# Hybrid block on one core: which engine writes the normalised rows of attention A

## The chip, the cores and the metric

One NeuronCore of one Trainium2 chip. The time is device microseconds (us) of one execution of the whole program, as the median of several runs. The program is a chain of four layers on 8 batches of 512 tokens with 128 features: linear attention A, a mixture of experts, a logarithmic attention B, and the mixture of experts once more. All of it is fp32.

## The reference, cut to what matters

```python
def layernorm(x, eps=1e-5):
    return (x - mean(x)) / sqrt(var(x) + eps)

def attn_a(x):                       # x is the normalised input, 8 x 512 x 128
    q, k, v = split(x @ W_qkv)       # 16 heads of 8
    q, k = rope(q), rope(k)
    q_feat, k_feat = elu(q * SCALE) + 1, elu(k) + 1
    kv, k_sum = k_feat.T @ v, k_feat.sum(tokens)
    out = (q_feat @ kv) / max(q_feat @ k_sum, 1e-6)
    return out @ W_out

x = x + attn_a(layernorm(x))
x = x + ffn(layernorm(x))            # shared expert + 2 of 8 experts
x = x + attn_b(layernorm(x))
x = x + ffn(layernorm(x))
```

The change concerns the first line of the chain alone: the layernorm in front of attention A.

## The kernel before, in words

Each engine (TensorE, VectorE, ScalarE, GpSimd, SyncE) has its own program, written out by hand, and runs it strictly in the order written. Semaphores tie the programs together: an instruction can raise one when it is done, and `wait_ge` holds an engine until one has reached a value. Nothing else sets the order of the work, so a wait holds up everything that stands behind it on its engine.

Attention A is a software pipeline over the 8 batches, in steps b = 1 to 9 (`A_STEPS`). In step b the engines finish the attention of batch b - 1 (named b in the calls below that ask for b > 1), work on the keys of the next, and prepare the queries of batch b + 1. x lies in SBUF as x_res, 4 tiles of 128 tokens per batch. A batch n is normalised like this:

- VectorE: statistics of the four tiles (`vector_stats`, L186), mean and variance into mean_var (L191), variance plus epsilon into var_eps (L193).
- GpSimd: rstd = var_eps to the power -0.5 (`pool_rstd`, L197).
- VectorE: four `tensor_scalar` of 128x128, x_hat = (x - mean) * rstd (`vector_hat`, L203). Mean and rstd are one number per partition (token). It waits for rstd and, so that x_hat is free again, for the transposes of the batch before (`turned`).
- TensorE: four transposes of x_hat (`tensor_turn`, L210); ScalarE copies the result to xT (L216), from which the projections read.

In step b TensorE's order is: tokens projected to v and k (L282), the router's logits of an earlier batch (L757), the sums of keys and values (`a_sums`, L249), the transposes of x_hat for batch b + 1 (`tensor_turn`, L210), the numerators (`a_numerators`, L256), the projection of q (L277, L278), transposes and the output projection (L266, L270). The numerators therefore stand behind the transposes, and the transposes wait for x_hat.

VectorE's order in step b (`a_vector_step`) is: the bias of the expert layer's norm (L1216, steps 3 to 6, waits for GpSimd's f_rstd), the four rows of x_hat (L203), `a_keep_heads` (L323, L324, waits for the sums), the rotation of k (L346), the router's logits (L1245), `a_divide` (L329, L331, L334, waits for the numerators), the features of q (L358), statistics of batch b + 2, the features of k (L358), the rotation of the next q (L346), the residual add (L341), and the statistics of the expert layer's norm (L1205 to L1210).

GpSimd's order in step b (`attn_a_pool`) is: the second half of the rotation of k (`a_add_turned`, L352), rstd of batch b + 2 (L197), the second half of the rotation of the next q (L352), f_rstd of the expert layer (L1029, in steps 2 to 5), and in steps 4, 5 and 6 a piece of preparation for the experts: a cast of 128x256 (L474) in step 4, a cast and a subtraction of 128x256 (L478, L480) in steps 5 and 6. After step 8 GpSimd sends the tokens to their experts by indirect DMA (L1047), as soon as VectorE has worked out the rows (rows_of, L1384).

Of the kernel before, what the change touches and what calls it, by code (L numbers as in the profile page):

```python
# [21 lines left out]
B, T, D = 8, 512, 128  # L22
H, HD = 16, 8
TT = T // 128
# [73 lines left out]
def build(nc, x_in, ins, out):  # L98

    ctx = ExitStack()  # L100
    with ctx:
        def sb(name, shape, dtype=F32):
            return ctx.enter_context(nc.sbuf_tensor(name, shape, dtype))

        def sem(name):
            return ctx.enter_context(nc.semaphore(name))
# [13 lines left out]
        mean_var = sb("mean_var", [128, TT, 2])  # L120
        var_eps = sb("var_eps", [128, TT])
        neg_half = sb("neg_half", [128, TT])
        rstd = sb("rstd", [128, TT])
        x_hat = sb("x_hat", [128, TT, D])
        xT = sb("xT", [128, T])

        def xs(n, t=0, tiles=1):

            return x_res[:, bass.ds((n - 1) * (TT * D) + t * D, tiles * D)]
# [6 lines left out]
        def signals(engine, prefix, passed=1.0, **steps):  # L136


            made = [(sem(f"{prefix}_{name}"), k) for name, k in steps.items()]
            starts[engine] += [(s, int(k * passed)) for s, k in made if int(k * passed)]  # L140
            return [s for s, _ in made]
# [29 lines left out]
        class Norm:  # L171
# [2 lines left out]

            def __init__(self, name, used, used_count, used_before=0):
                self.used, self.used_count, self.used_before = used, used_count, used_before
                self.stats_done, self.mean_done, self.var_ready, self.hat_ready = signals(
                    "vector", name, stats_done=TT, mean_done=TT, var_ready=1, hat_ready=TT)
                self.rstd_ready, = signals("pool", name, rstd_ready=1)
                self.turned, = signals("tensor", name, turned=1)  # L180
                self.xT_ready, = signals("scalar", name, xT_ready=1)
                self.go = sem(f"{name}_go")
# [13 lines left out]
                p.wait_ge(self.var_ready, n + 1)  # L196
                nc.gpsimd.tensor_tensor(rstd[:], var_eps[:], neg_half[:], ALU.pow).then_inc(self.rstd_ready, 1)  # L197

            def vector_hat(self, v, n):
                v.wait_ge(self.rstd_ready, n + 1)  # L200
                v.wait_ge(self.turned, n)
                for t in range(TT):
                    nc.vector.tensor_scalar(x_hat[:, t, :], xs(n, t), mean_var[:, t, 0:1], rstd[:, t:t + 1],  # L203
                                            ALU.subtract, ALU.mult).then_inc(self.hat_ready, 1)

            def tensor_turn(self, pe, n, to):
# [21 lines left out]
        na = Norm("a", a_kv, 1)  # L228
# [90 lines left out]
        def a_keep_heads(v, b):  # L319

            v.wait_ge(a_sum, b)
            v.wait_ge(a_num, b - 1)
            nc.vector.tensor_tensor(kv_bd[:, 0:D], bank(5, D), const["same_head"][:], ALU.mult).then_inc(a_bd, 1)  # L323
            nc.vector.tensor_scalar(kv_bd[:, D:D + H], const["head_mask"][:], psum[:, 5, D:D + 1], None,  # L324
                                    ALU.mult).then_inc(a_bd, 1)

        def a_divide(v, b):
            v.wait_ge(a_num, b)
            nc.vector.tensor_scalar(den[:], num_den(5)[:, :, D:D + H], EPS, None, ALU.max).then_inc(a_den, 1)  # L329
            v.wait_ge(a_den, b)  # L330
            nc.vector.reciprocal(rec[:], den[:]).then_inc(a_rec, 1)  # L331
            v.wait_ge(a_rec, b)
            v.wait_ge(a_oT, b - 1)
            nc.vector.tensor_tensor(o_tok[:].rearrange("p t (h d) -> p t h d", d=HD),  # L334
                                    num_den(5)[:, :, 0:D].rearrange("p t (h d) -> p t h d", d=HD),
                                    rec[:].unsqueeze(3).broadcast_to([128, TT, H, HD]),
                                    ALU.mult).then_inc(a_o, 1)
# [5 lines left out]
        def a_rotate(v, b, n, prod, first_bank, table):  # L343

            v.wait_ge(a_feat, 2 * b + n - 1)
            nc.vector.tensor_tensor(prod, psum[:, first_bank:first_bank + 2, :], table, ALU.mult).then_inc(a_prod, 1)  # L346

        def a_add_turned(p, b, n):

            prod = (q_prod, k_prod)[n]  # L350
            p.wait_ge(a_prod, 2 * b + n + 1)
            nc.gpsimd.tensor_tensor(prod[:, 0, :], prod[:, 0, :], prod[:, 1, :], ALU.add).then_inc(a_rope, 1)  # L352

        def a_feature(v, b, n, prod, e, feat):

            v.wait_ge(a_exp, 2 * b + n + 1)
            v.wait_ge((a_num, a_sum)[n], b)
            nc.vector.scalar_tensor_tensor(feat, prod[:, 0, :], 0.0, e, ALU.max, ALU.add).then_inc(a_feat, 1)  # L358
# [5 lines left out]
        def a_stats(v, n):  # L364
            v.wait_ge(loaded_x[min(n, 4) - 1], 16 * (B - 3) if n == 4 else 16)
            na.vector_stats(v, n)

        def a_vector_step(v, b):
            if 1 <= b - AHEAD <= ffn_1.early:
                ffn_1.vector_bias(v, b - AHEAD)  # L370
            if b < B:
                na.vector_hat(v, b + 1)
            if b > 1:
                a_keep_heads(v, b)
            if b <= B:
                v.wait_ge(a_kv, b + 1)
                a_rotate(v, b, 1, k_prod, 2, rope_k)
            if 1 <= b - AHEAD - 1 <= ffn_1.early:
                ffn_1.vector_logits_of(v, b - AHEAD - 1)
            if b > 1:  # L380
                a_divide(v, b)
            if b <= B:
                a_feature(v, b, 0, q_prod, q_exp, q_feat)
            if b == 7:
                ffn_1.vector_first(v, 0)
            if b == 8:
                ffn_1.vector_gates(v, 0)
                ffn_1.vector_pages(v, 0)
                ffn_1.vector_rows(v, 0)
            if b + 2 <= B:  # L390
                a_stats(v, b + 2)
            if b <= B:
                a_feature(v, b, 1, k_prod, k_exp, k_feat)
            if 1 <= b - AHEAD <= ffn_1.early:
                ffn_1.vector_low(v, b - AHEAD)
            if b < B:
                a_rotate_q(v, b + 1)
            if b == B + 1:
                ffn_1.vector_bias(v, ffn_1.first_late)
                ffn_1.vector_stats(v, ffn_1.first_late + 1)  # L400
            if b > 1:
                a_add(v, b)
            if 1 <= b - AHEAD + 1 <= ffn_1.early:
                ffn_1.vector_stats(v, b - AHEAD + 1)
            if b == 7:
                ffn_1.vector_second(v, 0)
            if b == 8:
                ffn_1.vector_stats(v, ffn_1.first_late)
                ffn_1.vector_experts(v, 0)

        def attn_a_vector(v):
            a_stats(v, 1)
            na.vector_hat(v, 1)
            v.wait_ge(loaded_first, 16 * len(first_loads))
            a_rotate_q(v, 1)
            a_stats(v, 2)
            for b in A_STEPS:
                a_vector_step(v, b)
# [39 lines left out]
        def attn_a_pool(p):  # L458

            na.pool_rstd(p, 1)  # L460
            a_add_turned(p, 1, 0)
            nc.gpsimd.memset(x_res[:, B * TT * D:], 0.0).then_inc(set_zero, 1)
            na.pool_rstd(p, 2)
            for b in range(1, B + 1):
                a_add_turned(p, b, 1)
                if b + 2 <= B:
                    na.pool_rstd(p, b + 2)
                if b < B:
                    a_add_turned(p, b + 1, 0)
                if 1 <= b - AHEAD + 1 <= ffn_1.early:  # L470
                    ffn_1.pool_rstd(p, b - AHEAD + 1)
                if b == 4:
                    p.wait_ge(loaded, 16 * len(rest_loads))
                    nc.gpsimd.tensor_copy(const["earlier"][:], earlier_room).then_inc(split_low, 1)  # L474
                if b in (5, 6):
                    g = b - 5
                    whole, high, low = w["w_expert"][:, g * INNER:(g + 1) * INNER], w_shared[:, g, 0, :], w_shared[:, g, 1, :]
                    nc.gpsimd.tensor_copy(high, whole).then_inc(split_high, 1)  # L478
                    p.wait_ge(split_high, g + 1)
                    nc.gpsimd.tensor_tensor(low, whole, high.bitcast(F32), ALU.subtract).then_inc(split_low, 1)  # L480
            sends = (0, 4, 8, 12, 14, 2 * ffn_1.tiles(0))
            for k in range(len(sends) - 1):
                ffn_1.send(p, 0, sends[k], sends[k + 1])
                if ffn_1.first_late + k <= B:
                    ffn_1.pool_rstd(p, ffn_1.first_late + k)
# [1945 lines left out]
```

## Time and profile before

| | |
|---|---|
| median of 3 runs | 1026.62 us (1026.45 to 1029.6) |
| profiled execution, its own time | 1028.43 us |
| its span, first to last instruction | 1026.6 us |
| busy share: TensorE, VectorE, ScalarE, GpSimd | 80%, 72%, 55%, 57% |
| attention A within it | 0 to about 125 us |

In the rows below PE is TensorE's matmul, PEld its weight load, DVE VectorE, ACT ScalarE, POOL GpSimd. L203 is line 203 of the kernel. In a timeline row the first number is the start in us, the second the duration of the group, x4 the number of instructions in it; in brackets stands how long the engine was idle before it and what it waited for ("issue" is a wait that the profile can't name).

### The profile page before, as it was taken

Reading aid. Unit: us, or ns where it says so; the run is one execution under the profiler, and the core shown is the slowest. Engines: PE = TensorE matmul, PEld = TensorE weight load, DVE = VectorE, ACT = ScalarE, POOL = GpSimd, SP = SyncE. Lnnn points to the kernel's source line nnn. Section 1 sums busy time; section 2 is a strip of 40 time slices with the busy share of each in tenths; the row PEclk is TensorE's granted clock in tenths of the full one; section 3 lists DMA queues with packets and bytes.
Section 4 is the critical chain, followed back from the end, with each engine's and each line's share of the span. In section 5 each row is a group of like instructions: output and inputs, shape, how many; then the busy total and the mean of one; then the engine's idle time right before and its main releaser. Section 6 shows DMA issues by size and latency. Waiting matters only on the chain. (4 is left out here: it accounts for less than half of the span.)

```text
span 1026.6 us, 19542 instructions
## 1 busy us (share of the span) xinstructions
PE 822.4 (80%) x6459; PEld 546.7 (53%) x6459; DVE 734.5 (72%) x1506; ACT 568.4 (55%) x805; POOL 589.0 (57%) x815
## 2 busy tenths in 40 slices
PE   4887587899997777888888888979795678899890
PEld 2676466798985333333333333333352267898880
DVE  3888845455564658899999998999779645565574
ACT  1454142233345577989898989998763251233230
POOL 2343585881274566665644444455317877788783
PEclk9899678999997787999999999999877598999996
DMA  9990012123338477474837473732210121132443
GB/s 270 303 131 1 19 36 72 52 81 114 101 92 239 140 215 225 121 221 127 227 100 220 111 226 104 231 99 63 62 42 24 34 75 39 40 102 81 135 136 119
DMA packets 114402, 124.00 MB, mean 121 GB/s; under 512 B 13329, under 2 KB 76561, under 8 KB 114177
## 3 DMA queue, kind: packets, MB, share of 16 engines
q1 hardware_dynamic: 96512, 100.80, 35.8%
q0 software_dynamic: 8416, 17.29, 5.4%
q10 hardware_dynamic: 9376, 4.65, 1.6%
q8 instruction: 56, 0.92, 0.4%
q14 instruction: 42, 0.34, 0.1%
HBM read 59.97 MB, written 62.72 MB: 120 GB/s over the span
## 5 line engine op out<-in xcount | busy, mean ns | idle before, releaser
L2070 DVE TENSOR_SCALAR ring_b<-psum 128x1024 int32<-128x1024 int32 x160 | 194.2, 1217 | 25.1 <-PE psum L1765 23.9
L1930 ACT ACTIVATE ring_a<-psum 128x1024 f32<-128x1024 f32 x160 | 162.4, 1021 | 47.3 <-PE psum L1765 45.8
L1936 ACT ACTIVATE ring_b<-ring_b 128x1024 f32<-128x1024 f32 x160 | 168.7, 1055 | 34.5 <-DVE ring_b L2070 34.1
L2198 POOL TENSOR_SCALAR_AFFINE_SELECT ring_b<-ring_b 128x512 f32<-128x512 f32 (+1 forms) x112 | 80.3, 730 | 171.6 <-ACT ring_b L1936 171.3
L1765 PE MATMUL psum<-stacks 32*128 32x128 f32 (+3 forms) x1024 | 99.8, 389 | 59.6 <-DVE ring_b L2070 39.8
L1765 PEld LDWEIGHTS psum<-stacks 32*128 32x128 f32 x1024 | 57.6, 195 | 164.6 <-ACT ring_a L1930 75.7
L2062 DVE TENSOR_SCALAR ring_a<-ring_a 128x1024 f32<-128x1024 f32 x160 | 119.3, 751 | 11.7 <-ACT ring_a L1930 11.7
L949 ACT ACTIVATE ring_b<-psum 128x512 f32<-128x512 f32 x72 | 42.6, 592 | 116.5 <-PE psum L834 116.5
L1818 PE MATMUL psum<-ring_b,values 128*32 128x256 f32 (+3 forms) x1024 | 96.5, 488 | 8.2 <-POOL ring_b L2198 8.2
L1797 PE MATMUL psum<-ring_a,ones_s 128*32 128x256 f32 (+3 forms) x1024 | 93.0, 473 | 10.1 <-POOL ring_a L2198 9.2
L1448 DVE TENSOR_TENSOR ring_b<-psum,ring_b 128x512 f32<-128x512 f32 x72 | 49.2, 683 | 67.7 <-ACT ring_b L949 67.7
L1092 POOL DMA_INDIRECT r_rows<-y_sorted,rows_of x64 | 67.4, 1053 | 51.8 <-DMA y_sorted<-y_out 39.5
L848 PE MATMUL psum<-w_expert,ring_b 128*128 x568 | 85.6, 285 | 13.8 <-ACT y_out L965 9.0
L2198 POOL TENSOR_SCALAR_AFFINE_SELECT ring_a<-ring_a 128x512 f32<-128x512 f32 (+1 forms) x112 | 79.6, 725 | 22.0 <-DVE ring_a L2062 21.9
L848 PEld LDWEIGHTS psum<-w_expert,ring_b 128*128 128x128 f32 x568 | 72.5, 193 | 21.3 <-issue 21.0
L1071 POOL DMA_INDIRECT y_token<-y_out,token_of x71 | 71.5, 1007 | 21.4 <-POOL pause_room L492 19.9
L1047 POOL DMA_INDIRECT x_sorted<-r_rows,rows_of x64 | 64.0, 1001 | 31.0 <-POOL pause_room L492 15.5
L834 PE MATMUL psum<-ring_a,ring_b 128*128 128x128 f32 x576 | 73.7, 283 | 5.3 <-issue 3.7
L492 POOL MEMSET pause_room<- 128x256 f32 x220 | 75.6, 344 | 0.2
L1047 POOL DMA_INDIRECT x_marked<-r_rows,rows_of x64 | 63.5, 992 | 18.9 <-POOL pause_room L492 16.0
L834 PEld LDWEIGHTS psum<-ring_a,ring_b 128*128 128x128 f32 x576 | 70.6, 200 | 6.4 <-issue 4.6
L834 PE MATMUL psum<-ring_a,v_tok 128*128 128x128 f32 x560 | 68.6, 275 | 0.0
(220 smaller groups left out, 1480.5 us busy)
## 6 DMA issues: line engine op xcount, KB each, us to landing
stack_q<-parts SPq DMA_DIRECT2D x32, 256.0 KB
stack_ky<-parts SPq DMA_DIRECT2D x32, 256.0 KB
stacks<-stack_q SPq DMA_DIRECT2D x64, 128.0 KB, 3.4
stacks<-stack_ky SPq DMA_DIRECT2D x64, 128.0 KB, 3.9
stack_k<-parts SPq DMA_DIRECT2D x32, 256.0 KB
stacks<-stack_k SPq DMA_DIRECT2D x64, 128.0 KB, 3.0
stack_qr<-parts SPq DMA_DIRECT2D x32, 256.0 KB
stacks<-stack_qr SPq DMA_DIRECT2D x64, 128.0 KB, 2.6
```

The lines of the kernel that those rows point to most:

```text
L492: nc.gpsimd.memset(pause_room[:], 0.0).then_inc(paused, 1)
L834: mm = nc.tensor.matmul(bank(2 * (k % 2) + g)[:, at:at + 128], w_pages[i % 4][:, g * INNER + c * 128:g * INNER + (c + 1) * 128], x_turned[ ...
L848: mm = nc.tensor.matmul(tiles(bank(4))[:, i % 4, :], hidden[:, self.items.index(("pair", j)) % 8, at:at + 128], w["w_expert"][:, bass.ds(s ...
L1047: nc.gpsimd.indirect_dma_start(out=out, out_offset=bass.IndirectOffsetOnAxis(ap=rows_of[:, n, at + t:at + t + 1], axis=0), in_=row, in_off ...
L1765: mm = nc.tensor.matmul(bank(2 * pair + j % 2)[:, column:column + width], keys[rows, s, kb * 128:(kb + 1) * 128], queries[rows, s, q0:q0 + ...
L1797: mm = nc.tensor.matmul(psum[32 * j:32 * j + 32, 4, q0:q0 + width], ones_s[:, s, :], exps[:, n % RING, j, column:column + width], start=i ...
L1818: mm = nc.tensor.matmul(psum[32 * j:32 * j + 32, into, q0:q0 + width], values[:, b % 2, kb, 4 * j + s, :], ring[:, m % RING, j, column:col ...
L1930: nc.scalar.activation(exps[:, n % RING, 2 * u:2 * u + 2, :], psum[:, first:first + 2, :], ACT.Exp, scale=SCALE).then_inc(self.exp, 1)
L1936: nc.scalar.activation(part, part, ACT.Ln, bias=1.0).then_inc(self.ln, 1)
L2062: nc.vector.tensor_scalar(part, part, CLIP_LO, CLIP_HI, ALU.max, ALU.min).then_inc(self.clip, 1)
L2070: nc.vector.tensor_scalar(ring[:, m % RING, HEADS_B[u][0]:HEADS_B[u][1] + 1, :].bitcast(I32), psum[:, first:first + 2, :].bitcast(I32), 0x ...
L2198: ins = nc.gpsimd.affine_select(out=part, in_=part, pattern=[[0, part.ap[1][1]], [1, 128]], compare_op=ALU.is_ge, fill=0.0, base=0, channe ...
```

## The change

The four instructions that write x_hat go from VectorE to GpSimd, with the same operands and the same two waits. On GpSimd they stand at the head of step b, in front of the second half of the rotation of k; for batch 1 they stand right behind its rstd. The semaphore hat_ready is now raised by GpSimd. Lines after L371 move up by two or three numbers.

```diff
@@ class Norm
-                self.stats_done, self.mean_done, self.var_ready, self.hat_ready = signals(
-                    "vector", name, stats_done=TT, mean_done=TT, var_ready=1, hat_ready=TT)
-                self.rstd_ready, = signals("pool", name, rstd_ready=1)
+                self.stats_done, self.mean_done, self.var_ready = signals(
+                    "vector", name, stats_done=TT, mean_done=TT, var_ready=1)
+                self.rstd_ready, self.hat_ready = signals("pool", name, rstd_ready=1, hat_ready=TT)
...
-            def vector_hat(self, v, n):
-                v.wait_ge(self.rstd_ready, n + 1)
-                v.wait_ge(self.turned, n)
+            def pool_hat(self, p, n):
+                p.wait_ge(self.rstd_ready, n + 1)
+                p.wait_ge(self.turned, n)
                 for t in range(TT):
-                    nc.vector.tensor_scalar(x_hat[:, t, :], xs(n, t), mean_var[:, t, 0:1], rstd[:, t:t + 1],
+                    nc.gpsimd.tensor_scalar(x_hat[:, t, :], xs(n, t), mean_var[:, t, 0:1], rstd[:, t:t + 1],
                                             ALU.subtract, ALU.mult).then_inc(self.hat_ready, 1)
@@ def a_vector_step(v, b)
-            if b < B:
-                na.vector_hat(v, b + 1)
@@ def attn_a_vector(v)
             a_stats(v, 1)
-            na.vector_hat(v, 1)
@@ def attn_a_pool(p)
             na.pool_rstd(p, 1)
+            na.pool_hat(p, 1)
             a_add_turned(p, 1, 0)
             nc.gpsimd.memset(x_res[:, B * TT * D:], 0.0).then_inc(set_zero, 1)
             na.pool_rstd(p, 2)
             for b in range(1, B + 1):
+                if b < B:
+                    na.pool_hat(p, b + 1)
                 a_add_turned(p, b, 1)
```

What this does to the order on GpSimd in steps 5 to 7 (- as before, + as changed):

```order
 L1029 TENSOR_TENSOR f_rstd<-f_var_eps,neg_half 128x4
 L474 CAST earlier<-values 128x256
+L203 TENSOR_SCALAR x_hat<-x_res,mean_var,rstd 128x128 x4
 L352 TENSOR_TENSOR ring_a<-ring_a 128x512
 L197 TENSOR_TENSOR rstd<-var_eps,neg_half 128x4
...
 L478 CAST w_shared<-w_expert 128x256
 L480 TENSOR_TENSOR w_shared<-w_expert,w_shared 128x256
+L203 TENSOR_SCALAR x_hat<-x_res,mean_var,rstd 128x128 x4
 L352 TENSOR_TENSOR ring_a<-ring_a 128x512
 L197 TENSOR_TENSOR rstd<-var_eps,neg_half 128x4
```

The rows of x_hat now stand behind f_rstd of the expert layer and behind the pieces for the experts, which GpSimd issues at the end of the step before.

On VectorE, at the head of each of the steps 3 to 6:

```order
 L1210 TENSOR_SCALAR f_var_eps<-f_mean_var 128x4
 L1216 SCALAR_TENSOR_TENSOR f_nbias<-f_mean_var,f_rstd 128x4
-L203 TENSOR_SCALAR x_hat<-x_res,mean_var,rstd 128x128 x4
 L323 TENSOR_TENSOR ring_b<-psum,same_head 128x128
 L324 TENSOR_SCALAR ring_b<-head_mask,psum 128x16
```

The bias is followed at once by the two instructions of `a_keep_heads`. TensorE's and ScalarE's orders are the same in both kernels.

## Rows read from the trace of the kernel before

**Rows 1.** Engines by stretch: start:end, length, busy PE, PEld, DVE, ACT, POOL, clock, DMA
```profile
42.00:97.00 55.00, 44.98 (x308) 36.73 (x308) 47.37 (x142) 28.14 (x56) 22.65 (x22) 0.97 0.68 101
```

**Rows 2.** Timeline, step 5
```profile
66.18 1.02 POOL L1029 TENSOR_TENSOR f_rstd<-f_var_eps,neg_half 128x4 f32<-128x4 f32 x1 [0.84 <-DVE f_var_eps L1210]
...
67.16 0.40 POOL L474 CAST earlier<-values 128x256 fp32r<-128x256 f32 x1
67.23 0.34 DVE L1216 SCALAR_TENSOR_TENSOR f_nbias<-f_mean_var,f_rstd 128x4 f32<-128x4 f32 x1 [1.13 <-POOL f_rstd L1029]
67.49 1.11 DVE L203 TENSOR_SCALAR x_hat<-x_res,mean_var,rstd 128x128 f32<-128x128 f32 x4
...
68.70 0.63 PE L210 MATMUL psum<-identity,x_hat 128*128 128x128 f32 x4 [1.20 <-issue]
...
70.35 0.23 DVE L329 TENSOR_SCALAR ring_b<-psum 128x64 f32<-128x64 f32 x1 [0.18 <-PE psum L256]
```

**Rows 3.** Timeline, steps 3 (first two) and 4
```profile
40.98 1.02 POOL L1029 TENSOR_TENSOR f_rstd<-f_var_eps,neg_half 128x4 f32<-128x4 f32 x1 [0.86 <-DVE f_var_eps L1210]
...
42.12 1.11 DVE L203 TENSOR_SCALAR x_hat<-x_res,mean_var,rstd 128x128 f32<-128x128 f32 x4
...
53.97 1.02 POOL L1029 TENSOR_TENSOR f_rstd<-f_var_eps,neg_half 128x4 f32<-128x4 f32 x1 [0.85 <-DVE f_var_eps L1210]
...
54.94 1.14 PE L249 MATMUL psum<-values,ring_a 128*128 128x129 f32 x8
...
55.10 1.12 DVE L203 TENSOR_SCALAR x_hat<-x_res,mean_var,rstd 128x128 f32<-128x128 f32 x4
...
57.97 0.22 DVE L329 TENSOR_SCALAR ring_b<-psum 128x64 f32<-128x64 f32 x1 [0.18 <-PE psum L256]
```

**Rows 4.** Prices: two copies in a row; GpSimd's copy and addition (ns min/median/max)
```profile
402.80 0.53 POOL L2211 COPY values<-v_tok 128x128 f32<-128x128 f32 x2
...
L2211 POOL COPY values<-v_tok x4: 282/287/814, 401.8 to 403.0; 128x128 f32<-128x128 f32 x4
...
L352 POOL TENSOR_TENSOR ring_a<-ring_a x13: 1264/1269/1276, 32.7 to 106.4; 128x512 f32<-128x512 f32 x13
```

**Rows 5.** Timeline, batch 1 (first two) and steps 1 and 2
```profile
6.78 1.11 DVE L203 TENSOR_SCALAR x_hat<-x_res,mean_var,rstd 128x128 f32<-128x128 f32 x4 [1.24 <-POOL rstd L197]
...
9.69 1.09 PE L210 MATMUL psum<-identity,x_hat 128*128 128x128 f32 x4 [9.69 <-DMA head_mask<-in_head_mask]
...
20.23 1.03 POOL L197 TENSOR_TENSOR rstd<-var_eps,neg_half 128x4 f32<-128x4 f32 x1
...
21.29 1.11 DVE L203 TENSOR_SCALAR x_hat<-x_res,mean_var,rstd 128x128 f32<-128x128 f32 x4 [1.15 <-POOL rstd L197]
...
23.46 0.68 DVE L358 SCALAR_TENSOR_TENSOR ring_a<-ring_a 128x512 f32<-128x512 f32 x1
23.62 1.64 POOL L352 TENSOR_TENSOR ring_a<-ring_a 128x512 f32<-128x512 f32 x1 [2.36 <-DVE ring_a L346]
...
28.54 1.30 POOL L352 TENSOR_TENSOR ring_a<-ring_a 128x512 f32<-128x512 f32 x1 [1.77 <-DVE ring_a L346]
...
31.70 0.66 PE L210 MATMUL psum<-identity,x_hat 128*128 128x128 f32 x4 [0.64 <-ACT values L436]
```

**Rows 6.** Timeline, steps 6 (first three) and 7
```profile
78.57 1.02 POOL L1029 TENSOR_TENSOR f_rstd<-f_var_eps,neg_half 128x4 f32<-128x4 f32 x1 [0.85 <-DVE f_var_eps L1210]
...
79.88 1.51 DVE L203 TENSOR_SCALAR x_hat<-x_res,mean_var,rstd 128x128 f32<-128x128 f32 x4
80.03 0.78 POOL L480 TENSOR_TENSOR w_shared<-w_expert,w_shared 128x256 fp32r<-128x256 f32 x1
...
90.93 0.73 POOL L480 TENSOR_TENSOR w_shared<-w_expert,w_shared 128x256 fp32r<-128x256 f32 x1
...
94.49 0.23 DVE L329 TENSOR_SCALAR ring_b<-psum 128x64 f32<-128x64 f32 x1
```

**Rows 7.** Timeline, after step 8: the start of GpSimd's sends
```profile
114.57 1.34 POOL L1047 DMA_INDIRECT x_sorted<-r_rows,rows_of  x1 [6.87 <-DVE rows_of L1384]
```

## The prediction

> **What bounds the kernel now.** I read the busy time by stretch first. In steps 3 to 7 of attention A VectorE is busy 47.4 of 55 us, GpSimd 22.7, TensorE 45.0 [rows 1]. So 1.1 us a step taken off VectorE looks like a gain, and GpSimd seems to have room. A busy share does not say what ends last, though, so I read the timeline of single steps next, at the place of the edit. Step 5 [rows 2] goes so: f_rstd on GpSimd ends at 67.20; VectorE, which had waited 1.13 us for it, does the bias and then the four rows of x_hat, until 68.60; TensorE, idle for 1.20 us, begins the transposes at 68.70; and VectorE's division (L329) begins at 70.35, after an idle 0.18 us, when the numerators are there. From the end of x_hat to the division is 1.75 us. In step 4 it is the same: x_hat ends at 56.22, the division begins at 57.97, again 1.75 us later [rows 3]. That is the chain to look at: f_rstd, x_hat, transposes, numerators (which stand behind the transposes on TensorE), division. Whatever VectorE does between x_hat and the division (keeping the heads, rotating k) must be done by then, but doing it earlier does not bring the division forward. Behind the division VectorE's order goes on to the next statistics, and so to the next f_rstd.
>
> So the time is decided by **when x_hat ends**, not by which engine is relieved. Last comes what lies behind: GpSimd waits 6.87 us for rows_of of VectorE before it can send the first tokens at 114.57 [rows 7]. GpSimd's chain of sends starts there, so I let a shift of attention A pass to the end in full.
>
> **The change, part by part.** VectorE loses four instructions in batch 1 and in steps 1 to 7: eight times 1.1 us or more. GpSimd gains the same 32 instructions. No DMA moves. The two waits go along: rstd is written by GpSimd itself one place or more ahead, and `turned` of the batch before has long been raised, since that batch was already projected; both cost about nothing. What is queued behind the four rows on GpSimd is the second half of the rotation of k, which has to wait for VectorE's rotation anyway.
>
> *Price h of the four rows on GpSimd.* The trace of before has no `tensor_scalar` on GpSimd, so I bound it. Nearest from below is its copy of 128x128: one takes 0.29 us, two in a row 0.53, hence one more every 0.24; four take 0.29 + 3 x 0.24 = 1.0 us [rows 4]. From above its two-tensor operations: 1.27 us for 512 columns [rows 4], about 0.75 for 256 [rows 6], so 0.52 for 256 columns and 0.49 for an operation of 128; four take 2.0. x_hat reads one tensor, as the copy does, but has two arithmetic operations and two numbers per partition to fetch. I take 0.4 a piece, above the middle: h = 1.6, between 1.0 and 2.0. VectorE does the four in 1.11 [rows 2].
>
> The Trainium skill (GPSIMD Engine Reference, section 8, Key points) says that for elementwise work VectorE is structurally about twice as fast. By that the four rows would take 2.2 us, an estimate from that page, and the sum below would be 7.8 us instead of 3.9. For one input the copy's row speaks against it (0.24 us a piece, where VectorE's x_hat takes 1.11 / 4 = 0.28); the operation itself no row here shows.
>
> *Step by step*, the end of x_hat before against the end with h = 1.6:
>
> - Batch 1: VectorE began at 6.78, when rstd was there; with h = 1.6 x_hat ends at 8.4 instead of 7.9, and TensorE waits until 9.69 for a weight's DMA [rows 5]. Nothing, up to h = 2.9.
> - Step 1: rstd ends at 21.26, x_hat ended at 22.40 [rows 5]; now 21.26 + 1.6 = 22.86. VectorE, without its wait of 1.15 and its 1.11 us, comes to the features of q (L358, an operation on two SBUF tensors) about 2.2 us earlier than its 23.46, which is in the middle of GpSimd's rows. How the two get along is seen at 23.46: L358 of 0.68 us had just begun, and GpSimd's addition took 1.64 us in place of 1.27 [rows 4, 5]. It was held until L358 ended. I add 0.6 (bounds 0 and 0.7). Loss 1.06. All that follows in steps 1 and 2 hangs on it: transposes, projection, rotation of q, its sum on GpSimd, the exponentials.
> - Step 2: x_hat now follows the addition of 28.54 + 1.30 on GpSimd: 29.84 + 1.6 = 31.4, where the transposes had waited until 31.70 for ScalarE's copy [rows 5]. Both shift alike; cover 0.3 us. Nothing.
> - Step 3: f_rstd ends at 42.00, x_hat ended at 43.23 [rows 3]; now 43.60. Loss 0.37.
> - Step 4: f_rstd ends at 54.99, x_hat ended at 56.22 [rows 3]; now 56.59. Loss 0.37.
> - Step 5: the cast stands between; it ends at 67.56, now 69.16 against 68.60 [rows 2]. Loss 0.56.
> - Step 6: cast and subtraction stand between, and end at 80.81; now 82.41 against 81.39 [rows 6]. Loss 1.02. Here the head of the step is 1.2 us later on GpSimd than on VectorE, whatever h is.
> - Step 7: the second subtraction ends at 91.66; now 93.26, and the division 1.75 later at 95.01 against 94.49 [rows 6]. Loss 0.52.
>
> Sum 1.06 + 0.37 + 0.37 + 0.56 + 1.02 + 0.52 = **3.9 us**. VectorE's saving stands in this sum at nothing: it becomes idle time in front of the division. Smaller holds of GpSimd by the tiny L1216 and L324, 0.1 or so a step, I leave out. With h = 1.0 each of the six falls by 0.6, except that step 4 gains nothing, since the sums of keys and values end only at 56.08 there and VectorE needs them before the numerators [rows 3], and step 7 returns to its old limit: 0.46 - 0.23 + 0 - 0.04 + 0.42 + 0 = 0.6 us. With h = 2.0: 3.9 + 6 x 0.4 + 0.1 in step 2 = 6.4 us.
>
> The profiled execution took 1028.43 us, of which 1026.6 are its span; it would become 1032.3. The median of the runs shown is 1026.62, lower by 1.8, and I forecast against it: 1026.62 + 3.9 = **1030.5 us**.
>
> **The rivals.**
>
> *Not slower: GpSimd's rows at the price of its copy.* h = 1.0 and the loss is 0.6: 1027.2 us. For it: one tensor input, like the copy. Against it: two more operands. It decides below h = 1.46, where the sum, 3.9 - 6 x 0.14, falls to 0.3% (3.1 us), about what a measurement of this kernel can tell from no change. Chance 0.2, and part of my forecast's own spread ends there too.
>
> *Twice VectorE's price or more.* h = 2.2, by the rows a little above the two-tensor addition: 3.9 + 6 x 0.6 + 0.3 in step 2 = 7.8, so 1034.4 us. For it: GpSimd's addition takes 1.27 us on 512 columns. Against it: the copy, which at 0.24 us a piece is no slower than VectorE's own rows of x_hat. Chance 0.2.
>
> *Faster: what VectorE is spared counts.* If the division did not hang on x_hat, seven steps of 1.1 us would come off: 7.8 us, 1018.8. For it: VectorE's 86% in steps 3 to 7. Against it: the 1.75 us repeated in steps 4 and 5, with the numerators behind the transposes on TensorE. It decides only where GpSimd has x_hat done well before VectorE had it, and GpSimd cannot begin before f_rstd ends, 1.2 to 1.4 us before VectorE was done in steps 3 to 5. Chance 0.07.
>
> *That the rows do not stand where the change says.* The order shows them on GpSimd, behind f_rstd and the casts, so they are there; but "head of the step" is later in time on GpSimd than on VectorE, which is in the sum. A remaining 0.03 goes to things not seen.
>
> **How the numbers follow.** Forecast 0.5, copy price 0.2, double price 0.2, freed VectorE 0.07, rest 0.03. The likeliest is 1030.5. The range goes from 1026.4, just under no change and the copy price, to 1035.0, just over the double price; outside it lie the freed VectorE and part of the rest, and a tail of each price. Slower by over 0.3%: 0.36 of the forecast's 0.5, 0.2 of the double price and a little of the rest: 0.57. Within: 0.14 + 0.2 + 0.01: 0.35. Faster: 0.08.
>
> **What would show it.** In the changed profile the four rows L203 on GpSimd should span 1.3 to 1.9 us, beginning right behind f_rstd in steps 3 and 4 and behind the cast or subtraction in steps 5 to 7; the division should come 1.75 us after their end in each; VectorE should be idle in front of it by about 1 us; and the first send should begin about 4 us later than 114.57. In step 1 the rows should be stretched by VectorE's L358. I am wrong if the division comes well before 1.75 us after x_hat (then VectorE's saving counts), if the rows take 1.0 us or over 2, or if the later part of the program does not carry the shift of the first send to the end.

## The result, and the profile after

The changed kernel takes 1047.89 us in the median (1046.25 to 1053.84, 4 runs) against 1028.11 us before (1026.45 to 1031.25, 4 runs). The ratio is 1.0212, 95% interval 1.0169 to 1.0254: slower by about 20 us. I had forecast slower, by 3.9 us, with 1035.0 as the upper end. The direction was right, the size wrong by a factor of five.

The first row to look at is the one that the trace of before could not have: the price of x_hat on GpSimd (ns min/median/max of one instruction).

```profile
L203 POOL TENSOR_SCALAR x_hat<-x_res,mean_var,rstd x32: 787/797/1319, 6.6 to 112.7; 128x128 f32<-128x128 f32 x32
```

0.79 us a row, where I had taken 0.4 and had put 0.49 as the upper bound [rows 4]. Step 5 of the changed kernel, in order of time, answers to [rows 2]:

```profile
77.64 1.02 POOL L1029 TENSOR_TENSOR f_rstd<-f_var_eps,neg_half 128x4 f32<-128x4 f32 x1 [0.85 <-DVE f_var_eps L1210]
...
78.62 0.40 POOL L474 CAST earlier<-values 128x256 fp32r<-128x256 f32 x1
78.69 0.34 DVE L1216 SCALAR_TENSOR_TENSOR f_nbias<-f_mean_var,f_rstd 128x4 f32<-128x4 f32 x1 [1.13 <-POOL f_rstd L1029]
79.01 3.14 POOL L203 TENSOR_SCALAR x_hat<-x_res,mean_var,rstd 128x128 f32<-128x128 f32 x4
...
82.25 0.63 PE L210 MATMUL psum<-identity,x_hat 128*128 128x128 f32 x4 [3.07 <-issue]
82.71 1.25 PE L256 MATMUL psum<-ring_b,ring_a 128*128 128x144 f32 x8
...
83.99 0.22 DVE L329 TENSOR_SCALAR ring_b<-psum 128x64 f32<-128x64 f32 x1 [3.12 <-PE psum L256]
```

The chain is the forecast one: f_rstd, cast, x_hat, transposes, numerators, division. x_hat ends at 82.15, the division begins 1.84 us later (1.75 before). What VectorE was spared, and the time by which x_hat comes later, stand as idle time in front of the division: 3.12 us in place of 0.18 [rows 2]. What differs from the forecast in this step is that x_hat takes 3.14 instead of 1.6 us.

Step 3 shows a second loss, which the forecast does not have:

```profile
47.10 3.14 POOL L203 TENSOR_SCALAR x_hat<-x_res,mean_var,rstd 128x128 f32<-128x128 f32 x4
...
50.34 1.09 PE L210 MATMUL psum<-identity,x_hat 128*128 128x128 f32 x4 [4.21 <-issue]
...
51.22 2.13 PE L256 MATMUL psum<-ring_b,ring_a 128*128 128x144 f32 x8
...
53.38 0.23 DVE L329 TENSOR_SCALAR ring_b<-psum 128x64 f32<-128x64 f32 x1 [4.60 <-PE psum L256]
```

Here the division comes 3.14 us after x_hat's end at 50.24, because the transposes take 1.09 and the numerators 2.13 us in place of 0.63 and 1.25. TensorE's clock says why (stretches of the changed kernel; the number behind the busy times is the granted clock, as a share of full speed):

```profile
47.00:50.30 3.30, 0.00 (x0) 0.00 (x0) 1.64 (x4) 0.03 (x1) 3.30 (x6) 0.88 1.22 163
50.30:53.40 3.10, 3.06 (x13) 3.09 (x14) 0.02 (x1) 1.94 (x5) 1.17 (x1) 0.50 1.25 147
...
82.20:84.00 1.80, 1.75 (x13) 1.79 (x14) 0.01 (x1) 1.09 (x3) 1.18 (x1) 0.89 0.00 0
...
98.20:101.30 3.10, 3.02 (x13) 3.05 (x14) 0.00 (x0) 1.90 (x5) 1.22 (x1) 0.50 0.03 5
```

TensorE does nothing from 47.0 to 50.3, waiting for x_hat, and works at 0.50, its lower level of 1.2 GHz, behind that. It is the same in steps 4 (0.52) and 6; in steps 5 and 7 the clock stays up and the 1.8 us hold. The length of the wait alone does not decide it: TensorE was idle for 2.14 us in front of the transposes in step 4, and for 3.07 in step 5.

Step 1 shows both the stretch that the forecast has (x_hat beside VectorE's L358) and a low clock that it does not have:

```profile
21.72 0.68 DVE L358 SCALAR_TENSOR_TENSOR ring_a<-ring_a 128x512 f32<-128x512 f32 x1
21.75 3.65 POOL L203 TENSOR_SCALAR x_hat<-x_res,mean_var,rstd 128x128 f32<-128x128 f32 x4
...
25.50 1.02 PE L210 MATMUL psum<-identity,x_hat 128*128 128x128 f32 x4 [4.96 <-issue]
```

The transposes took 0.63 us here in the kernel before. The clock is 0.53 from 25.4 to 28.5 and 0.50 from 28.5 to 32.0; in the kernel before it was 0.81 and 0.69 from 22.4 to 25.4 and from 25.4 to 29.0.

The loss is made in attention A and stays: the first send of GpSimd begins at 134.67 in place of 114.57 [rows 7], 20.1 us later.

```profile
134.67 1.38 POOL L1047 DMA_INDIRECT x_sorted<-r_rows,rows_of  x1 [6.86 <-DVE rows_of L1384]
```

### The profile page after: what moved, and what is told of

Its sections match the earlier page's. It is cut to its first block and busy times, and to the rows that moved or that the text cites. A ratio compares the mean times of both kernels' runs of the same rounds, so it can differ in the third digit from the quotient of the medians.

```text
span 1044.5 us, 19542 instructions
## 1 busy us (share of the span) xinstructions
PE 825.5 (79%) x6459; PEld 551.4 (53%) x6459; DVE 723.3 (69%) x1474; ACT 568.3 (54%) x805; POOL 614.0 (59%) x847
```

## The experiments

The theory after the first look: the chain and its steps are as forecast; the loss of 20 us is the price of a row (0.79 in place of 0.4) plus TensorE's clock behind the longer wait. The rivals: GpSimd's work costs wherever it stands, by quarrelling with VectorE over the memory; or VectorE's time sets the step after all.

The begin of the division in each step, and of the first send, in us, for the kernels that matter below ("filler" is e3_filler, "swap" e8_swap):

| step | before | changed | filler | swap |
|---|---|---|---|---|
| 2 | 33.37 | 38.47 | 38.37 | 33.81 |
| 3 | 45.08 | 53.38 | 51.87 | 44.38 |
| 4 | 57.97 | 69.42 | 65.96 | 55.78 |
| 5 | 70.35 | 83.99 | 80.41 | 67.19 |
| 6 | 83.15 | 101.32 | 95.77 | 78.99 |
| 7 | 94.49 | 115.25 | 109.82 | 90.39 |
| first send | 114.57 | 134.67 | 129.2 | 112.2 |

### What a row costs by itself (e1_prices)

```diff
 na.pool_rstd(p, 1)
+room = r_rows[:, 2100:3540]
+x0, m0, r0 = xs(1), neg_half[:, 0:1], neg_half[:, 1:2]
+nc.gpsimd.tensor_scalar(room[:, 0:128], x0, m0, r0, ALU.subtract, ALU.mult)
+nc.gpsimd.tensor_scalar(room[:, 128:256], x0, m0, r0, ALU.subtract, ALU.mult)
+nc.gpsimd.tensor_scalar(room[:, 256:384], x0, 0.5, 2.0, ALU.subtract, ALU.mult)
+nc.gpsimd.tensor_scalar(room[:, 384:512], x0, r0, None, ALU.mult)
+nc.gpsimd.tensor_scalar(room[:, 512:640], x0, 2.0, None, ALU.mult)
+nc.gpsimd.tensor_scalar(room[:, 640:672], x_res[:, 0:32], m0, r0, ALU.subtract, ALU.mult)
+nc.gpsimd.tensor_scalar(room[:, 672:1184], x_res[:, 0:512], m0, r0, ALU.subtract, ALU.mult)
+nc.gpsimd.tensor_copy(room[:, 1184:1312], x0)
+nc.gpsimd.tensor_tensor(room[:, 1312:1440], x0, x0, ALU.subtract)
```

> The kernel before, with nine extra GpSimd instructions on scratch memory at about 7 us, where GpSimd has nothing to do and VectorE is idle as well. What they write is not used. Theory A (the price is the instruction's own): a tensor_scalar of 128x128 with mean and rstd as per-partition operands takes 0.79 us here too, as in the changed kernel. Theory B (the price comes from VectorE, which shares a way to the memory, or from operands just written): 0.3 to 0.5 us here. If A, the other forms tell what costs: with two constants in place of the two operands, with one operation, with 32 and with 512 columns. If the columns cost, 512 columns take about four times as long as 128; if the instruction costs a fixed sum, 512 columns in one instruction are far below four of 128. Copy 0.29 us, subtraction of two 128x128 tensors about 0.5.

GpSimd's timeline, in the order of the edit:

```profile
6.44 0.80 POOL L463 TENSOR_SCALAR r_rows<-x_res,neg_half 128x128 f32<-128x128 f32 x1
7.24 0.89 POOL L464 TENSOR_SCALAR r_rows<-x_res,neg_half 128x128 f32<-128x128 f32 x1
8.11 0.63 POOL L465 TENSOR_SCALAR r_rows<-x_res 128x128 f32<-128x128 f32 x1
8.74 0.60 POOL L466 TENSOR_SCALAR r_rows<-x_res,neg_half 128x128 f32<-128x128 f32 x1
9.32 0.52 POOL L467 TENSOR_SCALAR r_rows<-x_res 128x128 f32<-128x128 f32 x1
9.84 0.47 POOL L468 TENSOR_SCALAR r_rows<-x_res,neg_half 128x32 f32<-128x32 f32 x1
10.29 2.06 POOL L469 TENSOR_SCALAR r_rows<-x_res,neg_half 128x512 f32<-128x512 f32 x1
12.31 0.28 POOL L470 COPY r_rows<-x_res 128x128 f32<-128x128 f32 x1
12.58 0.39 POOL L471 TENSOR_TENSOR r_rows<-x_res 128x128 f32<-128x128 f32 x1
```

Meanwhile on VectorE, which then does nothing until 13 us:

```profile
6.45 1.41 DVE L203 TENSOR_SCALAR x_hat<-x_res,mean_var,rstd 128x128 f32<-128x128 f32 x4 [1.24 <-POOL rstd L197]
```

The first two rows, 0.80 and 0.89 us, ran beside VectorE's x_hat (until 7.86), against what was expected, and so do not tell the theories apart. The instructions behind them ran with VectorE idle. There the same form grows from 0.47 to 2.06 us from 32 to 512 columns, 3.3 ns a column, on top of about 0.36 (0.47 - 32 x 3.3 ns), which makes 0.79 for 128 columns. So theory A: it is the instruction's own price, not contention. Constants in place of the two operands take off about 0.2, one operation instead of two again about 0.1. The subtraction of two tensors, which I had used as the upper bound, takes 0.39: on GpSimd the operation with per-partition operands is the dearer one, not the one with two tensors.

### The rows a step earlier on GpSimd (e2_early)

```diff
 na.pool_rstd(p, 2)
+na.pool_hat(p, 2)
 for b in range(1, B + 1):
-    if b < B:
-        na.pool_hat(p, b + 1)
     a_add_turned(p, b, 1)
     if b + 2 <= B:
         na.pool_rstd(p, b + 2)
+        na.pool_hat(p, b + 2)
```

> The changed kernel, with GpSimd's four rows of x_hat right behind the rstd that they need, a step earlier, in place of at the head of the step behind f_rstd. Price and number of the instructions are the same. Theory A (x_hat's end is what counts): the transposes no longer wait for x_hat from step 2 on; only batch 1, step 1 and some delay of what stands behind the rows on GpSimd remain. 1028 to 1035 us, most of the loss of 20 us gone. Theory B (GpSimd's 25 us more of work, or its quarrel with VectorE over the memory, is the cost wherever it stands): 1042 us or more.

1038.84 us in the median, ratio 1.0117 (1.0051 to 1.0184); first send at 126.0. About half of the loss goes with the same instructions at the same price (the first send comes 8.7 us earlier than in the changed kernel), so the place matters, and theory B falls; but 10 us stay, where theory A had 0 to 7. Step 5 shows one part of where they come from:

```profile
72.11 1.27 POOL L352 TENSOR_TENSOR ring_a<-ring_a 128x512 f32<-128x512 f32 x1
73.34 1.03 POOL L1029 TENSOR_TENSOR f_rstd<-f_var_eps,neg_half 128x4 f32<-128x4 f32 x1
...
74.40 0.34 DVE L1216 SCALAR_TENSOR_TENSOR f_nbias<-f_mean_var,f_rstd 128x4 f32<-128x4 f32 x1 [2.50 <-POOL f_rstd L1029]
75.23 0.42 PEld L210 LDWEIGHTS psum<-identity,x_hat 128*128 128x128 f32 x4 [2.20 <-ACT values L433]
```

x_hat is early now, and the transposes wait for ScalarE's copy. But the 3.1 us of rows push what stands behind them on GpSimd: the rotation of q (L352), for which that copy waits, and f_rstd, for which VectorE waits 2.50 us in place of 1.13. Moved forward, the price is paid at another place of the same loop. Another part is the clock: in steps 3 and 6 it was 0.50 and the transposes and numerators took 1.11 and 2.13 us, in step 5 0.66 and 1.15. How the 10 us divide between the two was not measured.

### TensorE kept at work before x_hat comes (e3_filler, e9_after_again, e10_filler_again)

```diff
 pe.wait_ge(a_v, b + 1)
+for _ in range(2 if 1 < b < 7 else 0):
+    nc.tensor.matmul(bank(7), w["w_a"][:, 0:D], xT[:], start=True, stop=True)
 na.tensor_turn(pe, b + 1, 7)
```

> The changed kernel, with two extra projections (their result is overwritten) on TensorE in front of its wait for x_hat in steps 2 to 6. Theory A (part of the loss is TensorE's clock, which was granted at 0.5 for about 3 us behind the wait in steps 3, 4 and 6): the clock stays up, the way from x_hat's end to the division falls from 3.1 to about 1.8 us in these three steps, and the time is 3 to 5 us below the changed kernel's, so about 1043 to 1045. Theory B (the clock there covers nothing that is waited for, or does not follow the idle time): no gain, 1047 to 1049.

1046.41 us, ratio 1.0178 (1.0122 to 1.0234), first send at 129.2. In attention A it is theory A: from step 3 to the first send 5.5 us are won (table). At the end it lies between the two theories and could not be told from the scatter, so I ran it again beside the changed kernel.

> The changed kernel as it is, beside the next one on the same chip. Both theories: 1046 to 1050 us, first send at 134 to 135.

> The changed kernel with two extra projections in front of TensorE's wait for x_hat in steps 2 to 6, once more and beside the changed kernel itself. In the first look its first send came at 129.2 instead of 134.7, but the program ended only 1.5 us earlier, within the scatter of the runs. Theory A (the 5 us won by the clock in attention A reach the end, and that execution lost them to chance later): the first send again at about 129, and the median 3 to 6 us below the changed kernel's of the same call. Theory B (they are given back later): first send at about 129, medians within 2 us.

1049.08 us for the changed kernel (ratio 1.0210, 1.0164 to 1.0256) and 1043.99 with the filler (1.0174, 1.0123 to 1.0224), first sends at 134.4 and 129.2. The medians differ by 5.1 us, as the first sends do; the intervals of the two ratios overlap, but five of the six executions with the filler took less than any of the six without it. That is theory A. Step 3 with the filler (e10), and its clock:

```profile
47.06 1.98 PE L302 MATMUL psum<-xT,w_a 128*128 128x512 f32 x4 [0.95 <-ACT values L435]
...
50.26 0.66 PE L210 MATMUL psum<-identity,x_hat 128*128 128x128 f32 x4 [1.21 <-POOL x_hat L203]
...
50.75 1.15 PE L256 MATMUL psum<-ring_b,ring_a 128*128 128x144 f32 x8
...
51.93 0.23 DVE L331 TENSOR_SCALAR ring_b<-psum 128x64 f32<-128x64 f32 x1 [3.17 <-PE psum L256]
```

```profile
47.00:50.30 3.30, 2.03 (x5) 0.72 (x5) 1.64 (x4) 0.01 (x1) 3.30 (x6) 1.00 1.18 212
50.30:53.40 3.10, 3.10 (x16) 2.14 (x17) 1.40 (x4) 2.45 (x6) 1.14 (x1) 1.00 1.23 161
```

With 2 us of useless work in front of the wait the clock is 1.00 behind it, the numerators take 1.15 instead of 2.13 us, and x_hat's end (50.20) to the division is 1.73 us. More work on TensorE brings the first send forward by 5 us in both looks, and the end by as much between the medians of the second.

The changed kernel itself, seen a second time in e9, had its low clock partly in other places: the numerators took 1.98 us in step 5 and 2.13 in step 7, where they had taken 1.25 and 1.15. Its first send came at nearly the same time as before (134.4 and 134.67). Behind which waits the clock is low thus changes from one execution to the next, and what decides it was not tested.

### VectorE's spared time given back (e5_refill)

```diff
+if b < B:
+    nc.vector.tensor_tensor(r_rows[:, 2100:3124].rearrange("p (a n) -> p a n", a=2), psum[:, 2:4, :],
+                            rope_k, ALU.mult)
 a_rotate(v, b, 1, k_prod, 2, rope_k)
```

> The changed kernel, with one extra operation of 1.22 us on VectorE (on the rotation's inputs, into scratch) in front of the rotation of k in steps 1 to 7, so that VectorE gets back the time it was spared. Theory A (what VectorE is spared only becomes waiting in front of the division): no change against the changed kernel, ratio to the kernel before 1.018 to 1.024. Theory B (the spared time counts): 7 x 1.2 = 8.5 us more, ratio about 1.029.

1048.03 us, ratio 1.0207 (1.0147 to 1.0266), first send at 134.1. Theory A: seven times 1.22 us more on VectorE cost nothing. What VectorE was spared is not on the path of the changed kernel.

### The prediction's own price (e6_narrow)

The first 32 columns of each row alone are written, the rest of x_hat stays zero, so the result is another one.

```diff
-nc.gpsimd.tensor_scalar(x_hat[:, t, :], xs(n, t), mean_var[:, t, 0:1], rstd[:, t:t + 1],
+nc.gpsimd.tensor_scalar(x_hat[:, t, 0:32], x_res[:, bass.ds((n - 1) * (TT * D) + t * D, 32)], mean_var[:, t, 0:1], rstd[:, t:t + 1],
                         ALU.subtract, ALU.mult).then_inc(self.hat_ready, 1)
...
+nc.gpsimd.memset(x_hat[:], 0.0).then_inc(setup, 1)
```

> The changed kernel, but GpSimd writes only the first 32 of the 128 columns of each row of x_hat; the other 96 columns stay zero, so that the layer computes something else with the same work. By the price run a row then costs 0.45 us, four rows h = 1.8, near the 1.6 that the prediction took. Theory A (the prediction's sum is right and only its price was wrong): x_hat's end and the division are 1.75 to 1.85 us apart in all steps, TensorE's clock stays up, and the first send moves by 3.9 + 6 x 0.2 = 5.1 us against the kernel before, to about 120 (between 118.5 and 121.5); the time is 1031 to 1036. Theory B (place and order cost more than the sum has, whatever the price): first send at 125 or later.

1037.83 us in the median, scattered from 1029.94 to 1042.18; ratio 1.0102 (1.0034 to 1.0170). First send at 123.4, so 8.8 us later than before and between the two theories. The four rows take 1.83 us, as meant. In steps 3 and 4 the clock stays up, and their divisions lose 0.5 and win 0.1 us on top of what came before, where the sum with this price has 0.6 each. Step 5 does not hold:

```profile
69.72 1.83 POOL L203 TENSOR_SCALAR x_hat<-x_res,mean_var,rstd 128x32 f32<-128x32 f32 x4
71.62 0.72 PEld L210 LDWEIGHTS psum<-identity,x_hat 128*128 128x128 f32 x4 [2.22 <-issue]
...
72.53 2.13 PE L256 MATMUL psum<-ring_b,ring_a 128*128 128x144 f32 x8
...
74.70 0.22 DVE L329 TENSOR_SCALAR ring_b<-psum 128x64 f32<-128x64 f32 x1 [3.37 <-PE psum L256]
```

Behind a wait of 2.1 to 2.2 us the clock was 0.53 here, and the division comes 3.15 us after x_hat. That costs 1.3 us. Behind step 7 another 1.7 are lost: the wait for rows_of is 8.61 us in place of 6.87 [rows 7], with the clock at 0.50 from 116.0 to 123.0. Without these two losses 5.8 of the 8.8 us remain, near the 5.1 of theory A. So even near the price that I assumed, the forecast of 3.9 us would have been too low, for the most part by the clock. The other way round, 1.3 us less for the four rows brought the first send 11.3 us forward (134.67 - 123.4).

### x_hat taken out of the chain (e7_scalar, e8_swap)

In e7 ScalarE writes x_hat for batches 4 to 8 a step earlier:

```diff
+def vector_nbias(self, v, n):
+    v.wait_ge(self.rstd_ready, n + 1)
+    nc.vector.scalar_tensor_tensor(nbias[:], mean_var[:, :, 0], -1.0, rstd[:], ALU.mult, ALU.mult
+                                   ).then_inc(self.go, 1)
+
+def scalar_hat(self, a, n):
+    a.wait_ge(self.go, n - 3)
+    a.wait_ge(self.turned, n)
+    for t in range(TT):
+        nc.scalar.activation(x_hat[:, t, :], xs(n, t), ACT.Identity, bias=nbias[:, t:t + 1],
+                             scale=rstd[:, t:t + 1]).then_inc(self.hat_s, 1)
```

> The kernel before, but x_hat of batches 4 to 8 is written by ScalarE as x * rstd + (-mean * rstd), four operations of about 0.48 us, a step earlier, where ScalarE waits 3.5 us for the rotation of q; VectorE adds one tiny operation for -mean * rstd behind the rotation of the next q. Theory A (the chain f_rstd, x_hat, transposes, numerators, division is what a step hangs on): x_hat is no longer in the chain, the division comes earlier by about 1 us in steps 3, 5 and 6 and by less in steps 4 and 7; first send at 110 to 113 against 114.6, time 2 to 4 us below the kernel before. Theory B (VectorE's work or the sums of keys set the step): no change, within 1 us.

1025.09 us, ratio 0.9970 (0.9938 to 1.0003), first send at 112.3. The steps behave as in theory A (the division of step 6 at 79.13 instead of 83.15), but the total is just not told from no change.

In e8 two calls on VectorE are exchanged:

```diff
+if b < B:
+    na.vector_hat(v, b + 1)
 if 1 <= b - AHEAD <= ffn_1.early:
     ffn_1.vector_bias(v, b - AHEAD)
-if b < B:
-    na.vector_hat(v, b + 1)
```

> The kernel before with two calls exchanged: VectorE writes x_hat in front of the bias of the expert layer's norm, in the 1.13 us in which it otherwise waits for f_rstd. Theory A (no quarrel over the memory): the rows of x_hat hide in that wait, 1 us less in each of steps 3 to 6, 3 to 4 us in all. Theory B (a VectorE operation from memory to memory and a GpSimd one hold each other off, as the rows of x_hat in steps 2, 6 and 7 show it): x_hat and f_rstd come one after the other, in all 0 to 1.5 us less.

1023.19 us in the median of 12 runs against 1027.71 of 23 runs before, ratio 0.9960 (0.9927 to 0.9993). Step 6:

```profile
75.24 1.12 DVE L203 TENSOR_SCALAR x_hat<-x_res,mean_var,rstd 128x128 f32<-128x128 f32 x4
...
75.41 1.06 POOL L1029 TENSOR_TENSOR f_rstd<-f_var_eps,neg_half 128x4 f32<-128x4 f32 x1 [0.85 <-DVE f_var_eps L1210]
...
76.50 0.34 DVE L1216 SCALAR_TENSOR_TENSOR f_nbias<-f_mean_var,f_rstd 128x4 f32<-128x4 f32 x1
76.52 0.47 PEld L210 LDWEIGHTS psum<-identity,x_hat 128*128 128x128 f32 x4
...
78.99 0.23 DVE L329 TENSOR_SCALAR ring_b<-psum 128x64 f32<-128x64 f32 x1
```

VectorE's four rows stand inside the time in which GpSimd makes f_rstd, and neither is much longer for it (1.12 and 1.06 us; 1.11 and 1.02 in step 5 before [rows 2]). That is theory A: 4.1 us are won up to the division of step 7 (table). Of these 1.7 are lost again before the first send, where the clock was 0.50 from 105.0 to 112.2. In steps 4 to 7 VectorE no longer waits in front of the division: once x_hat has left the chain, VectorE's own order is what comes last there. The program is 0.4% faster than the kernel before, by an interval that only just leaves out no change.

## Why the prediction was right or wrong

- **The chain** (f_rstd, x_hat, transposes, numerators, division; VectorE's saving counts nothing): right. 1.73 to 1.84 us from x_hat to the division wherever the clock is up, 3.12 us of idle VectorE in front of the division, and refilling it costs nothing. The rival of the freed VectorE is refuted for this change by e5_refill.
- **The price h**: the term that failed. The prediction said "I take 0.4 a piece, above the middle: h = 1.6, between 1.0 and 2.0"; it measured 0.79 and h = 3.13, above the upper end, and above the 2.2 of the rival "twice VectorE's price or more" too. The nearest rows were chosen by the number of tensors that an instruction reads; what sets GpSimd's price here is the kind of the operation. The Trainium skill's factor of two for elementwise work (GPSIMD Engine Reference, section 8, Key points), which the prediction carried beside its sum, gave an estimate of 2.2. The trace agrees that GpSimd is the slower one, but by more: 3.13 against 1.11 on VectorE is a factor of 2.8.
- **The steps of the sum**: close once h is put in, the total more so than the single terms. With h = 3.13 the prediction's own lines give 0.2 for batch 1 (6.78 + 3.13 = 9.91, past the weight's DMA at 9.69), 2.6 in step 1, 1.2 in step 2 (its cover of 0.3 is gone), 1.9, 1.9, 2.1, 2.6 and 2.1 in steps 3 to 7: 14.6 us. With the filler, which keeps the clock up in steps 3 to 6, the first send moved by 14.6 (129.2 - 114.57). That the two are equal is partly luck. By the table the filler's division is 5.0 us late in step 2, where the lines have 4.0; it loses 1.8, 1.2, 2.1, 2.6 and 2.7 more in steps 3 to 7; and 0.7 comes back before the first send.
- **What VectorE's L358 does to the rows in step 1**, 0.6 us: right for the execution shown, where they took 3.65 in place of 3.13. In e9 and with the filler L358 ended 0.1 us before the rows began, and they took 3.13.
- **TensorE's clock**: no term of the sum, and the second failure. A longer wait for x_hat can cost more than its own length; behind it TensorE worked at 0.50 for some 3 us in steps 3, 4 and 6. What the filler took back of that is 134.67 - 129.2 = 5.5 us of the 20.1 at the first send. The filler does not stand in step 1, where the clock was 0.50 with it as well (24.9 to 28.0), so a part of the other 14.6 us is the clock's too; no run separates it.
- **The shift passes to the end**: right within the scatter. 20.1 us at the first send, 19.8 between the medians. From the first send to the end of the span, the ten executions whose first sends stand here took 905 to 919 us (912.0 before, 909.8 changed), so one execution alone could not show it.

## What to carry to other kernels

When work goes to another engine, the price of just that form of instruction on that engine has to be measured first; a bound from other kinds of operation is none, and nine scratch instructions in a place where both engines idle settle it in one run. Look for the wait that the moved work ends, not for the busiest engine: the same four rows, kept on VectorE but exchanged with the instruction that waits for GpSimd, hide in a wait that was there already. And a wait that grows in front of TensorE can be paid twice, once as time and once as clock.

## What the runs showed of the hardware that was not expected

- On GpSimd a `tensor_scalar` with two per-partition operands costs about 0.36 us plus 3.3 ns a column (0.47 us at 32, 0.80 at 128, 2.06 at 512 columns); a subtraction of two 128x128 tensors costs 0.39, a copy 0.28.
- GpSimd's power on 128x4 (f_rstd) and VectorE's four `tensor_scalar` on 128x128, both from memory to memory, ran beside each other nearly without holding each other up (1.06 and 1.12 us in e8), while GpSimd's addition of 128x512 stretched VectorE's rows to 2.07 us in step 2 of the kernel before, and VectorE's L358 stretched GpSimd's rows to 3.65 in step 1 of the changed one.
- How long TensorE was idle does not alone tell the clock behind it: 0.89 after 3.07 us in step 5 of the changed kernel, 0.53 after 2.06 us in step 5 of e6.
- Executions of one kernel scatter by several us, more than the 0.3% that the prediction counts on: the kernel before took from 1019.01 to 1033.79 us in one set of runs. In the first filler run the last stretch of the logarithmic attention (662.0 to 796.4) took 134.4 us at a clock of 0.85, in the changed kernel the corresponding one (672.0 to 797.5) 125.5 us at 0.90. What decides this from one execution to the next stays open.
